# Decoder layer: attention gates computed inside the recurrence and sent through DRAM, attention output unrolled by batch

## What is computed

```python
a = sigmoid(x @ Wa.T + ba); beta = sigmoid(x @ Wb.T + bb)
def step(St, inp):                      # one token, H = 16 heads, state 128x128 a head
    Sk = einsum('bhij,bhj->bhi', St, kt)
    err = Sk - vt
    Sn = at[..., None] * St - (bt[..., None] * err)[..., None] * kt[:, :, None, :]
    ot = einsum('bhij,bhj->bhi', Sn, qt)
_, outs = scan(step, S0, ...)           # 128 tokens
o = (out - mu) * rsqrt(var + 1e-05) * ln_g + ln_b
g = sigmoid(x @ Wg.T)                   # the gates: 2048 tokens x 16 heads x 128
o = (o * g).reshape(B, S, H * DV)
x1 = layernorm(x + o @ Wo.T)
```

## Time and profile before

| | us |
|---|---|
| median of three executions | 2637.16 (2631.98 to 2641.57) |
| span of the profiled execution | 2627.1 |
| projections, 0 to 671.9 | 671.9 |
| recurrence, 671.9 to 1852.6 | 1180.7 |
| attention output, 1852.6 to 2145.2 | 292.6 |
| long convolution and experts, to the end | 481.9 |

### The profile page before, as it was taken

The page is one execution under the profiler, slowest core; times in us unless marked ns, Lnnn a source line. Parts: engine busy times, 40 slices in busy tenths (PEclk is TensorE's granted clock), DMA queues, the critical chain, the costliest instruction groups (busy, mean ns, idle before and its releaser), DMA issues. The chain is left out here.

```text
span 2627.1 us, 38958 instructions
## 1 busy us (share of the span) xinstructions
PE 2046.5 (78%) x11890; PEld 1407.9 (54%) x11890; DVE 1781.7 (68%) x4427; ACT 1176.3 (45%) x2737; POOL 943.5 (36%) x976
## 2 busy tenths in 40 slices
PE   7999999999366776666676664557799959889994
PEld 4555555555255555554554543436678843456673
DVE  5777877777477777876777785838555517784444
ACT  2555555555355555554554453435233310223452
POOL 1443444444422222222222222220344425344773
PEclk8999999999588888877787777777899979999996
DMA  2656666665346778898999999975232233116985
GB/s 90 125 116 121 124 118 121 123 122 116 95 128 163 197 209 221 234 235 232 247 269 271 298 283 266 302 227 150 85 89 88 88 137 93 42 41 204 315 228 142
DMA packets 637357, 443.50 MB, mean 169 GB/s; under 512 B 290581, under 2 KB 590581, under 8 KB 631925
## 3 DMA queue, kind: packets, MB, share of 16 engines
q1 hardware_dynamic: 522776, 269.31, 39.6%
q0 software_dynamic: 41248, 130.60, 19.0%
q10 hardware_dynamic: 73152, 41.45, 5.3%
HBM read 238.76 MB, written 194.04 MB: 165 GB/s over the span
## 5 line engine op out<-in xcount | busy, mean ns | idle before, releaser
L950 ACT ACTIVATE p_diag_o<-p_ident,p_gd 128x128 f32<-128x128 f32 x1152 | 360.9, 389 | 314.0 <-PE p_ps_o L906 312.5
L387 DVE SCALAR_TENSOR_TENSOR p_y<-p_ps_proj,p_w,p_y 128x508 f32<-128x508 f32 (+2 forms) x576 | 415.8, 740 | 114.2 <-ACT p_y L301 100.6
L906 PE MATMUL p_ps_o<-p_ws,p_diag_o 128*128 128x128 f32 x1792 | 335.9, 349 | 166.2 <-ACT p_diag_o L950 84.3
L906 PEld LDWEIGHTS p_ps_o<-p_ws,p_diag_o 128*128 128x128 f32 x1792 | 296.2, 250 | 232.5 <-DVE p_ws L636 84.1
L237 PE MATMUL p_ps_proj<-p_x,p_w 128*128 128x512 f32 x768 | 341.5, 594 | 2.7 <-ACT p_beta_t L292 2.7
L865 PE MATMUL p_ps_z<-p_turned,p_gcol 112*32 112x128 f32 x3584 | 151.8, 305 | 225.7 <-DMA p_turned<-history 225.2
L201 POOL TENSOR_TENSOR p_kq<-p_y,p_sig 128x512 f32<-128x512 f32 x128 | 162.4, 1273 | 376.3 <-ACT p_sig L312 375.6
L865 PEld LDWEIGHTS p_ps_z<-p_turned,p_gcol 112*32 112x32 f32 x3584 | 98.6, 120 | 288.6 <-DMA p_turned<-history 253.7
L586 DVE SCALAR_TENSOR_TENSOR p_zo<-p_ws,p_gd,p_zo 128x128 f32<-128x128 f32 x768 | 239.1, 345 | 3.4
L580 DVE TENSOR_TENSOR p_ws<-p_ws,p_dec 128x128 f32<-128x128 f32 (+2 forms) x192 | 118.9, 619 | 174.1 <-PE p_ps_o L906 174.0
L237 PEld LDWEIGHTS p_ps_proj<-p_x,p_w 128*128 128x128 f32 x768 | 141.6, 191 | 157.2 <-issue 153.9
(11 more groups left out here) (260 smaller groups left out, 3830.3 us busy)
## 6 DMA issues: line engine op xcount, KB each, us to landing
gram<-p_gram SPq DMA_DIRECT2D x64, 512.0 KB
p_w<-in_wguT SPq DMA_DIRECT2D x64, 480.0 KB
history_sums<-p_sums ACTq DMA_DIRECT2D x112, 256.0 KB, 5.3
p_zo<-history_sums POOLq DMA_DIRECT2D x28, 1024.0 KB, 11.4
history<-p_hist SPq DMA_DIRECT2D x9, 2048.0 KB, 13.7
history<-p_late SPq DMA_DIRECT2D x9, 2048.0 KB, 14.2
decays<-p_dec SPq DMA_DIRECT2D x64, 256.0 KB, 2.3
beta_v<-p_bv SPq DMA_DIRECT2D x64, 256.0 KB, 2.5
```

The source lines that it names most:

```text
L387: nc.vector.scalar_tensor_tensor(out=yv[:, :, s:], in0=pv[:, :, 0:T - s], scalar=par[j % 2][:, kind, TAPS - 1 - s:TAPS - s], in1=yv[:, :, ...
L906: nc.tensor.matmul(ps_o[s // 4 % 2][:, s % 4, :], diag_o[p // DO % NDO][:, p % DO, :], rows[:, r, :], start=(s % 4 == 0 and r == 0), stop= ...
L950: last = nc.scalar.activation(diag_o[n % NDO][:, p % DO, :], ident[:], ACT.Copy, scale=gd[g][:, r, s:s + 1])
```

## The change

The gates leave the attention output. They are computed in the recurrence, as 64 blocks of one head by 512 tokens (two matmuls of 128x512 and one sigmoid each), and stored to a DRAM tensor `gates` of 16.8 MB. Leaf 0 takes 16 blocks, one before each step's `own_rows`, leaves 1 to 6 take 8 each, before the steps of the second half. x is loaded once, into the part of `late` that group 1's history does not use yet, by `projections`; Wg lies in the unused part of `hist[0]`, loaded by SP at the start of the recurrence. History rows are placed with an offset (`slot`) so that these parts are overwritten last. The blocks share the two PSUM buffers `ps_z` with the history sums.

The attention output becomes a pipeline by batch, fully unrolled, with three buffers for `o`, four PSUM banks for the transposes, and the residual of batch n-2 behind the normalisation of batch n. The gates of a pair come from DRAM in one load of 2 MB: two pairs' at the end of the recurrence, in place of x and Wg, the other six in the stage. The last stages keep their code.

```diff
+    GATES = [C] + 6 * [HALF] + (LEAVES - 7) * [0]
@@ recurrence, SP
+            sp.dma_start(wg, wgT.rearrange("(k p) c -> p k c", p=P)).then_inc(late_in, DMA)
             sp.wait_ge(cleared, CLEARED)
...
-            sp.dma_start(xT_sb, xT.rearrange("(k p) t -> p k t", p=P)).then_inc(late_in, DMA)
-            sp.dma_start(wg, wgT.rearrange("(k p) c -> p k c", p=P)).then_inc(late_in, DMA)
             sp.dma_start(wo, woT.rearrange("(h i) n -> i h n", i=DH)).then_inc(late_in, DMA)
+            for p in range(PB):
+                sp.dma_start(gate[p], gate_dram[p]).then_inc(late_in, DMA)
@@ recurrence, PE
+            def gate_product(at, j):
+                entry = gate_entry(at, j)
+                h, q = divmod(sum(GATES[:at]) + j, TOK // GATE_COLS)
+                if entry == 0:
+                    pe.wait_ge(late_in, DMA)
+                if entry >= NZ:
+                    pe.wait_ge(z_cp, entry - NZ + 1)
+                for k in range(KT):
+                    last = nc.tensor.matmul(ps_z[entry % NZ][:].rearrange("p q i -> p (q i)"), wg[:, k, h * DH:(h + 1) * DH],
+                                            x_sb[:, k, q * GATE_COLS:(q + 1) * GATE_COLS], start=(k == 0), stop=(k == KT - 1))
+                last.then_inc(gate_mm, 1)
...
                 for s in range(HALF, C):
+                    if gate_at(at, s) >= 0:
+                        gate_product(at, gate_at(at, s))
                     own_rows(at, s)
@@ recurrence, ACT
+            def gate_block(at, j):
+                entry, n = gate_entry(at, j), sum(GATES[:at]) + j
+                h, q = divmod(n, TOK // GATE_COLS)
+                act.wait_ge(gate_mm, n + 1)
+                if n >= NG:
+                    act.wait_ge(gate_saved[n % NG], n // NG * DMA)
+                nc.scalar.activation(gate_out[n % NG], ps_z[entry % NZ][:].rearrange("p q i -> p (q i)"),
+                                     ACT.Sigmoid).then_inc(z_cp, 1)
+                act.wait_ge(z_cp, entry + 1)
+                act.dma_start(gate_dram[2 * q:2 * q + 2, :, h].rearrange("p i b t -> i p (b t)"),
+                              gate_out[n % NG].rearrange("i (p t) -> i p t", p=2)).then_inc(gate_saved[n % NG], DMA)
...
                 for s in range(HALF, C):
                     made = past(s, made)
+                    if gate_at(at, s) >= 0:
+                        gate_block(at, gate_at(at, s))
                     if s == HALF + 3 and at + 1 < LEAVES:
                         near_blocks(at + 1)
@@ attention_out, SP
+            def load_o(n):
+                if n >= 3:
+                    sp.wait_ge(normed, n - 2)
+                if n == B // 2:
+                    sp.wait_ge(last_out, DMA * NCHUNK)
+                sp.dma_start(o[n % 3][:], o_dram[n, :, :, 0:DH].rearrange("h t i -> t h i")).then_inc(o_in[n % 3], DMA)
+            def load_x(n):
+                if n >= 2:
+                    sp.wait_ge(added, n - 1)
+                sp.dma_start(xr[n % 2][:], x[n]).then_inc(x_in[n % 2], DMA)
...
+            for n in range(3, B):
+                load_o(n)
+                if n % PB == 0:
+                    p = n // PB
+                    sp.wait_ge(gated, (p - 1) * PB)
+                    sp.dma_start(gate[p % 2], gate_dram[p]).then_inc(gate_in[p % 2], DMA)
+                load_x(n - 1)
@@ attention_out, PE
-            with pe.Fori(1, PAIRS - 1) as p:
-                heads(p)
-                turn_x1(p - 1)
-                gates(p + 1)
-                project(p)
...
+            for n in range(B + LAG + 2):
+                if n < B:
+                    heads(n)
+                if 0 <= n - LAG - 2:
+                    turn_x1(n - LAG - 2)
+                if 1 <= n <= B:
+                    project(n - 1)
@@ attention_out, POOL
+            for n in range(B):
+                if n + 1 < B:
+                    head_std(n + 1)
+                apply_gates(n)
+                if n >= LAG:
+                    row_std(n - LAG)
@@ attention_out, DVE (LAG = 2)
+            head_stats(0)
+            for n in range(B + LAG + 1):
+                if n + 1 < B:
+                    head_stats(n + 1)
+                if n < B:
+                    normalize(n)
+                if 0 <= n - LAG - 1:
+                    finish(n - LAG - 1)
+                if 0 <= n - LAG < B:
+                    residual(n - LAG)
```

More of the change, by code:

```diff
@@ L480, in recurrence @@
         late_in = m.sem("p2_late_in")
+        gate_mm = m.sem("p2_gate_mm")
+        gate_saved = [m.sem(f"p2_gate_saved{i}") for i in range(NG)]
         zo_zero = m.sem("p2_zo_zero")
@@ L1141, in _ @@
+            load_x(B - 1)
+            for i in range(2):
+                sp.wait_ge(x1_out[i], DMA * B // 2)
+                sp.wait_ge(x1t_out[i], DMA * B // 2)
         @block.gpsimd
```

401 lines of the change are left out of this document (181 added, 220 removed).

## The result

The changed kernel takes 2661.92 us in the median of four runs (2650.58 to 2676.24); the kernel before, run beside it, 2634.57 us (2620.62 to 2641.57). The ratio is 1.010, with a 95% interval from 1.0066 to 1.0134: about 1% slower. The forecast was 2646 us, 0.34% slower, with a range of 2617 to 2675. The time lies in the range and the sign is right. But the two halves of the sum are both off, and the larger one for a reason that the prediction had not seen.

The account below looks back on a forecast made before the run. It took PE to bound attention output and a DVE-PE-ACT chain the recurrence. Span 2627.1 + 31 (recurrence) - 22 (attention output) = 2636.1 us, plus 10.1 between span and median: 2646 us, range 2617 to 2675.

Parts of the forecast that it names:

- The direct cost of a second half: Recurrence, leaves 0 to 6: gate blocks ahead of PE's row products delay DVE 2.4 us a leaf, 17 us in all.
- Leaf 0: Recurrence, first half of leaf 0: eight more gate blocks cost 5 us, bounds 2.4 and 8.
- The load of Wg at nothing: Start of the recurrence: the 2 MB load lies beside POOL's 20 us of clearing buffers and costs nothing.
- The lag of ACT and PE: Recurrence, leaf ends: blocks on ACT delay PE's last products, the next leaf absorbs most; 6 us, bounds 0 and 10.
- the stores: Recurrence: 16.8 MB of gate stores on ACT's queue, priced by DMA engine time, cost 3 us, bounds 0 and 8.
- that load is tied to the end of DVE's leaf: Next leaf's first half: the history load comes only 2.4 us late, so PE's 4.46 us wait shrinks and absorbs lag.
- I take full clock: Recurrence, second halves: with gate blocks PE is nearly always busy, so a block is priced at full clock, 1.77 us.
- The recurrence as a whole: Whole recurrence stage: 31 us longer, bounds 15 and 61.
- the lag is carried: Rival, recurrence: ACT's 5.4 us a leaf are not absorbed, as history waits move with the leaf; 2666 us, chance 0.18.
- Attention output: Attention output stage: the load of o sets a 16.4 us batch period instead of 17.4; 22 us shorter, bounds 33 and 8.
- PE at half clock: Rival, attention output: PE at half clock needs 23 us a batch, 79 us more, 2725 us; chance 0.04.
- the rule: Trainium skill, cited against the change: a PE waiting for DMA between bursts drops its clock and pays in the next burst.

Follow-up runs that it names:

- gates_off: Changed kernel without the 64 gate blocks in the recurrence, attention output multiplying by a block of x instead, Wg load kept; 2594.82 us, ratio 0.9897 to the kernel before.
- x_late: Changed kernel with the load of x in attention output issued one batch later on SP's queue; 2631.36 us, ratio 1.001 to the kernel before.
- dve_gates: Kernel x_late with attention output's gate product on DVE instead of GpSimd; 2615.67 us, ratio 0.9933 to the kernel before.
- near_spread: Kernel dve_gates plus the store of o behind the loads of v, gram rows and beta, and ACT's near factors spread over steps 11 to 15; 2585.42 us, ratio 0.9817.

## Why the prediction was right, and where it was not

- **The direct cost of a second half (2.4 us a leaf): right.** For leaves 1 to 6 that is 14.4 us, and 14.3 us were measured, in each leaf 1.7 to 1.8 us at the gap of step 9 to 10 and 0.6 at the next. Moving the blocks behind the rows took it away, as the reasoning said.
- **Leaf 0 (5 us, and 2.4 for its second half): right, and a little high.** 5.9 us to its last step, 0.7 of them from the later start of the stage. The load of Wg at nothing holds: in `gates_off`, which has it, the first step of leaf 0 is 5.6 us later, but leaf 1 starts at 751.4 us, against 751.0 before.
- **The lag of ACT and PE (6 us) and the stores (3 us): wrong.** For leaves 1 to 6 the two gave 3 us and most of 3, some 6; the stretches grew by 30. The step that failed is "that load is tied to the end of DVE's leaf, which is only 2.4 us late; so PE's wait shrinks". The tie exists for the load of the first tiles. But ACT's last copy also releases the store of `o`, and its copy of the history releases the load of `v`, both on GpSimd's queue. I followed the lag along PE and DVE and never along that queue. The lag itself was of the size forecast: 2.7 us at each boundary and 1.6 more by step 2, 4.3 against 5.5 (though the lower clock adds 1.4 to 1.9 us to the seventh block on the way to it, which "I take full clock" had ruled out). And the first half can swallow it: with the store of `o` moved away, the six stretches are 3.3 us longer than before, for which the two terms had given some 6. The queue's order is thus the other 27 us (297.9 less 271.2). That it is the order is shown; which packets hold up the history is not.
- **The stores (3 us, bounds 0 and 8): too small.** Without them the stretches are 11 us shorter and the time some 31 us, more than the traces place. I priced the time of the 16 DMA engines, and neither the moment at which the stores run nor what they do to ACT. How the 11 us divide between traffic and ACT's work is not shown.
- **The recurrence as a whole: 50.9 us**, within the bounds of 15 and 61 and at the rival "the lag is carried" (46 to 51), though not by its mechanism. It was not ACT's lag that each leaf carried, since the first half did take it up.
- **Attention output (22 us): right in mechanism, short in size (29.1 us).** DVE waits about 5 us a batch for `o`, PE is busy 66% of the stage (70% forecast). The period is 15.3 us instead of 16.4. Half of the difference is the load of `o`, which reached DVE after 5.6 to 5.8 us (1947.56 to 1953.20, 1962.73 to 1968.52) and not 6.3; the other half is what stands ahead of it, 9.5 us from the statistics to the issue of `o` (1953.20 to 1962.73) and not 10.0. The gate load behind it, issued at 1948.04, holds nothing up in that turn. Stage 263.5 us against 270.
- **PE at half clock: no rival.** The clock of the stage fell from 0.98 to 0.80, and a turn's 16 transposes took 1.9 to 3.7 us. With 34% of its time to spare PE did not set the pace: the period fell to 13.6 and 12.7 us in `x_late` and `dve_gates`, at clocks of 0.83 and 0.86. The row of the last projection, which the prediction took as agreeing with the rule, shows one wait of 1.98 us, for POOL and not a DMA, and a granted clock of 0.89 in the 15.9 us behind it.
- **The time.** The two misses offset each other in part: 50.9 - 29.1 + 0.1 = 21.9 us where the sum had 9. The forecast was 16 us low, 13 of them in the span, and the unread queue alone would have been 27. That the time lies in the range is in part luck: the range reached up for a carried lag, which did not happen, and so had room for a cost that the prediction had not priced.

What one would have had to look at: every release that ACT gives at a leaf's end, and for each the queue behind it. The rows of GpSimd above show the store of `o` waiting 2.56 us for ACT already before the change.

## What to carry to other kernels

When an engine is made late, follow each semaphore that it releases, the ones that free a DMA on another queue above all, and ask what runs at the new moment of that transfer: here a wait that looked absorbed came back, because a transfer of 1 MB left 3.5 us later. In a loop with slack in one place, a local saving is only worth what the next limit allows: the near factors spread and the gate blocks behind the rows each did locally what was expected and neither alone moved the time. A bulk transfer that waits on a shared queue for an engine that has become late deserves a place of its own in the order: here moving the 1 MB of `o` behind the loads was worth 1.7%, though the loads themselves left hardly earlier. And small DVE operations have to be looked at beside GpSimd's large ones before a multiplication is left there "for free".

## What the runs showed of the hardware

- A 0.19 us operation of DVE took 3.1 to 4.0 us in twelve batches of `x_late`, beside GpSimd's product of two tiles of 128x2048. The normalisation, one input and two columns of scalars, is held up too. While the changed kernel fills its pipeline, 16 of them take 8.47 us beside GpSimd's 4.49 us, against 4.19 alone:

```profile
1925.77 8.47 DVE L1349 TENSOR_SCALAR p_on<-p_o,p_hm,p_hr 128x128 f32<-128x128 f32 x16 [0.15 <-DVE p_hr L1143]
1926.33 4.49 POOL L1246 TENSOR_TENSOR p_y<-p_y,p_late 128x2048 f32<-128x2048 f32 x1 [5.84 <-ACT p_y L1309]
1930.79 2.90 POOL L1239 TENSOR_TENSOR p_hr<-p_hr,p_neg_half 128x16 f32<-128x16 f32 x1
```

  The statistics were not held up (3.19 us in both cases), and DVE's operations beside the power of 128x16 (2.90 us on GpSimd) showed no further delay.
- While GpSimd's queue moved 1.03 MB in 4 us of `near_spread`, SP's queue, with history tiles asked for, moved one packet. The Trainium skill ("DMA: Bandwidth & Descriptors", section "Queues, rings and completion order") has each DMA engine take turns between queues packet by packet, by which SP's queue should have had a share. The trace does not show whether its packets were ready in these 4 us, so it neither bears this out nor refutes it.
- In the changed kernel a PE that had been busy at full clock stood for 2.85 and shortly after for 1.09 us; it was granted 0.52 in the 3.3 us behind, and a gate block took 3.48 us instead of 1.88. A wait does not always do this: in `near_spread` PE stood for 1.88 us at the same place of leaves 2 and 3, and the gate block behind it took 3.22 us in leaf 2 and 1.88 us in leaf 3.
